# Batch 0's experts through the turned path, and five of the shared expert's low parts on VectorE

## The reference

```python
x = x + _L0_cond_ref(...)     # dense plus a low-rank mix over 8 experts
x = x + _L1_cond_ref(...)     # masked weights mixed by cond_8, plus bias
x = x + _L2_cond_ref(...)     # MoE: softmax, top 2 of 8, gated MLP 128 -> 512 -> 128, plus a shared expert
x = x + _L3_cond_ref(...)     # argmax expert, silu-gated MLP 128 -> 256 -> 128
# the gated MLP of the third layer:
def _gemma_mlp(x, gate_w, up_w, down_w):
    g = jnp.einsum('bsh,hi->bsi', x, gate_w)
    u = jnp.einsum('bsh,hi->bsi', x, up_w)
    return jnp.einsum('bsi,ih->bsh', jax.nn.gelu(g, approximate=True) * u, down_w)
```

## Time and profile before

| what | value |
|---|---|
| median of 3 runs | 81.27 us (81.17 to 81.83) |
| the profiled execution | 81.71 us, its span 80.3 us |
| PE busy | 76.7 us, 95% of the span |
| DVE, ACT, POOL busy | 52.1, 47.3, 45.4 us |
| bytes moved | 21.65 MB, mean 269 GB/s |

### The profile page before, as it was taken

How to read it: one execution, slowest core, us unless ns; L and a number is a source line. 1 busy time by engine, 2 the same in 40 slices (tenths; PEclk the granted TensorE clock), 3 DMA queues, 4 the chain that set the end, 5 groups by cost and what they waited for, 6 DMA issues and landing times.

```text
span 80.3 us, 1611 instructions
## 1 busy us (share of the span) xinstructions
PE 76.7 (95%) x500; PEld 69.4 (86%) x500; DVE 52.1 (65%) x116; ACT 47.3 (59%) x95; POOL 45.4 (57%) x44
## 2 busy tenths in 40 slices
PE   6999999999999999999995999999999999999990
PEld 6978998888888998999882989989989999999990
DVE  1489569869756637387697939499398465157371
ACT  6420796798855898637999059356450522168260
POOL 3021356298999999999999999995600000000000
PEclk9999999999999999999999999999999999999999
DMA  1999489999999993499988999999989789600202
GB/s 14 317 345 386 58 324 352 407 419 422 431 394 414 386 407 123 70 379 359 386 223 208 361 341 318 270 315 328 309 302 303 243 215 269 237 14 0 65 0 65
DMA packets 8791, 21.65 MB, mean 269 GB/s; under 512 B 976, under 2 KB 5200, under 8 KB 8784
## 3 DMA queue, kind: packets, MB, share of 16 engines
q1 hardware_dynamic: 8496, 20.77, 74.8%
q10 hardware_dynamic: 288, 0.79, 2.5%
HBM read 17.88 MB, written 0.52 MB: 229 GB/s over the span
## 4 chain that ended last, share of the span: by engine, by line
PE 87%; DMA 4%; SPq 2%; DVE 2%; ACT 1%; issue 1%
PE bank L961 18%; PE bank L934 9%; PE bank L976 8%; PE bank L991 5%; PE bank L897 5%; PE bank L913 5%; PE bank L905 5%; DMA x_t<-p 4%; PE bank L944 4%; PE bank L947 4%; PE bank L945 4%; PE bank L836 4%; PE bank L828 4%; SPq L259 2%; PE bank L921 2%; PE bank L923 2%
## 5 line engine op out<-in xcount | busy, mean ns | idle before, releaser
L418 ACT ACTIVATE gelu<-bank 128x512 f32<-128x512 f32 x24 | 14.2, 594 | 11.5 <-PE bank L947 6.9
L361 POOL TENSOR_TENSOR pair_low<-pair_w,wide_h 128x512 fp32r<-128x512 f32 x14 | 17.8, 1297 | 0.9 <-ACT wide_h L456 0.9
L691 DVE SCALAR_TENSOR_TENSOR hid<-gelu,wsel,bank 128x512 f32<-128x512 f32 x16 | 11.8, 736 | 7.6 <-PE bank L947 2.0
L366 POOL TENSOR_TENSOR hid_l<-hid,hid_h 128x512 fp32r<-128x512 f32 x8 | 10.3, 1295 | 2.0 <-ACT hid_h L469 1.9
L944 PE MATMUL bank<-wide_h,x_h 128*128 128x512 f32 x24 | 9.8, 409 | 0.0
L428 ACT ACTIVATE half<-bank,half_bias 128x128 f32<-128x128 f32 x12 | 3.8, 365 | 9.5 <-PE bank L976 6.5
L945 PE MATMUL bank<-wide_h,x_l 128*128 128x512 f32 x24 | 9.4, 390 | 0.0
L705 DVE STREAM_TRANSPOSE p<-hid 128x512 f32<-128x512 f32 x12 | 8.5, 712 | 0.8 <-DMA x_t<-p 0.4
L456 ACT ACTIVATE wide_h<-pair_w 128x512 fp32r<-128x512 f32 x14 | 8.1, 622 | 0.1
L689 DVE TENSOR_TENSOR hid<-gelu,bank 128x512 f32<-128x512 f32 x8 | 5.5, 686 | 3.8 <-POOL hid_l L366 2.7
L934 PE MATMUL bank<-x_t,pair_w 128*128 128x128 f32 x64 | 7.5, 275 | 0.0
(11 more groups left out here) (120 smaller groups left out, 162.9 us busy)
## 6 DMA issues: line engine op xcount, KB each, us to landing
pair_w<-in_skill SPq DMA_DIRECT2D x11, 768.0 KB, 7.4
w<-in_layer SPq DMA_DIRECT2D x6, 384.0 KB, 9.5
x_t<-p SPq DMA_DIRECT2D x12, 128.0 KB, 3.6
b_mix<-p SPq DMA_DIRECT2D x12, 128.0 KB, 4.3
shared_sb<-in_skill SPq DMA_DIRECT2D x1, 768.0 KB, 11.8
home_x<-in_skill SPq DMA_DIRECT2D x1, 768.0 KB, 12.6
home_h<-in_skill SPq DMA_DIRECT2D x1, 768.0 KB, 4.3
home_l<-in_skill SPq DMA_DIRECT2D x1, 768.0 KB, 6.3
```

The source lines that it names most:

```text
L361: pool.tensor_tensor(low_of(b, k)[:, m, :], w[:, m, :], wide_h[:, ring_at(b, k) % RING, m, :].bitcast(fp32), ALU.subtract).then_inc(wide_l ...
L366: pool.tensor_tensor(hid_l[:, k % 3, :], hid[:, k % 2, :], hid_h[:, k % 3, :].bitcast(fp32), ALU.subtract).then_inc(hid_low, 1)
L418: act.activation(gelu[:, n, :], ps[:, :], ACT.Gelu_apprx_tanh).then_inc(gelu_ready, 1)
L691: dve.scalar_tensor_tensor(hid[:, n, :], gelu[:, n, :], wsel[:, bass.DynSlice(weight, 1)], u_ps[n][:, :], ALU.mult, ALU.mult).then_inc(hid ...
```

## The change

`TURNED` becomes 0 to 6, so that batch 0's experts take the wide form, with its rounding, low parts, transposes and swap; batch 7 stays plain as it was. POOL makes the low parts of the shared expert's hidden values only for k = 0, 1, 2 (`POOL_LOW = 3`), DVE those for k = 3 to 7 (`hidden_rest`), each with a semaphore of its own. ACT rounds batch 0's and batch 1's weights during the shared expert, one part in each of seven places. The steps of batches 0 to 4 stand in another order on PE, ACT and DVE. On SP `swap(0)` stands ahead of the load of (4, 1), and `swap(1)` behind that one load, where it stood behind three before.

```diff
--- before.py
+++ after.py
@@ -24,7 +24,8 @@
 PAIRS, THIRD = 7, 3
 RING = 4
 IN_BANK = 4
-TURNED = range(1, B - 1)
+TURNED = range(B - 1)
+POOL_LOW = 3
 
 
 HEAD = 2 * C + B + B * E
@@ -280,10 +282,7 @@
 
                 pick(0, 0)
                 load(0, 0)
-                for b, k in ((1, 0), (0, 1), (1, 1)):
-                    pick(b, k)
-                    load(b, k)
-                for b, k in ((2, 0), (2, 1), (3, 0)):
+                for b, k in ((0, 1), (1, 0), (1, 1), (2, 0), (2, 1), (3, 0)):
                     pick(b, k)
                     load(b, k)
                 pick(3, 1)
@@ -298,15 +297,15 @@
                 for b in range(5, B):
                     pick(b, 0)
                     pick(b, 1)
+                swap(0)
                 sp.wait_ge(down_done, NSH)
                 load(4, 1)
+                swap(1)
                 load(5, 0)
                 load(5, 1)
-                swap(1)
-                sp.wait_ge(down_done, down_at(0, 0))
-                load(6, 0)
                 swap(2)
                 sp.wait_ge(down_done, down_at(0, 1))
+                load(6, 0)
                 load(6, 1)
                 swap(3)
                 sp.wait_ge(down_done, down_at(1, 0))
@@ -364,19 +363,15 @@
                 def hidden_low_part(k):
                     pool.wait_ge(hid_high, k + 1)
                     pool.tensor_tensor(hid_l[:, k % 3, :], hid[:, k % 2, :], hid_h[:, k % 3, :].bitcast(fp32),
-                                       ALU.subtract).then_inc(hid_low, 1)
-
-                for k in range(3):
-                    hidden_low_part(k)
-                wide_low_part(1, 0, 0)
-                hidden_low_part(3)
-                hidden_low_part(4)
-                wide_low_part(1, 0, 1)
-                hidden_low_part(5)
-                hidden_low_part(6)
-                wide_low_part(1, 1, 0)
-                hidden_low_part(7)
-                wide_low_part(1, 1, 1)
+                                       ALU.subtract).then_inc(hid_low_pool, 1)
+
+                wide_low_part(0, 0, 0)
+                hidden_low_part(0)
+                hidden_low_part(1)
+                wide_low_part(0, 0, 1)
+                hidden_low_part(2)
+                wide_low_part(0, 1, 0)
+                wide_low_part(0, 1, 1)
                 for b in TURNED[1:]:
                     for k in range(TOP_K):
                         for m in range(2):
@@ -468,40 +463,40 @@
                         act.wait_ge(down_done, k - 2)
                     act.activation(hid_h[:, k % 3, :], hid[:, k % 2, :], ACT.Copy).then_inc(hid_high, 1)
 
+                rounds = {1: (0, 0, 1), 3: (0, 1, 0), 4: (0, 1, 1), 5: (1, 0, 0), 6: (1, 0, 1), 7: (1, 1, 0)}
+                round_part(0, 0, 0)
                 gelu_step(0, 0, shg_ps[0])
                 for k in range(1, NSH):
                     gelu_step(k, k % 2, shg_ps[k % 3])
                     round_hidden(k - 1)
-                    if k in (3, 4):
-                        round_part(1, 0, k - 3)
-                    if k == NSH - 1:
-                        round_part(1, 1, 0)
+                    if k in rounds:
+                        round_part(*rounds[k])
+                expert_gelu(0, 0)
                 round_hidden(NSH - 1)
-                expert_gelu(0, 0)
                 round_part(1, 1, 1)
                 expert_gelu(0, 1)
                 round_pair(2, 0)
                 round_pair(2, 1)
                 expert_gelu(1, 0)
+                expert_gelu(1, 1)
                 round_pair(3, 0)
-                expert_gelu(1, 1)
+                expert_gelu(2, 0)
                 round_pair(3, 1)
-                expert_gelu(2, 0)
-                halve3(0)
-                tanh_step(0)
                 expert_gelu(2, 1)
                 round_pair(4, 0)
                 expert_gelu(3, 0)
                 round_pair(4, 1)
                 expert_gelu(3, 1)
+                halve3(0)
+                tanh_step(0)
+                expert_gelu(4, 0)
                 round_pair(5, 0)
-                expert_gelu(4, 0)
+                expert_gelu(4, 1)
                 round_pair(5, 1)
-                expert_gelu(4, 1)
-                round_pair(6, 0)
                 halve3(1)
                 tanh_step(1)
                 expert_gelu(5, 0)
+                round_pair(6, 0)
                 expert_gelu(5, 1)
                 round_pair(6, 1)
                 halve3(2)
@@ -681,15 +676,20 @@
 
                     dve.wait_ge(gelu_ready, k + 1)
                     dve.wait_ge(u_done, k + 1)
-                    if 2 <= k < NSH + 2:
-                        dve.wait_ge(hid_low, k - 1)
-                    elif NSH + 2 <= k < NSH + 4:
-                        dve.wait_ge(down_done, down_at(0, n))
+                    if 2 <= k < POOL_LOW + 2:
+                        dve.wait_ge(hid_low_pool, k - 1)
+                    elif POOL_LOW + 2 <= k < NSH + 2:
+                        dve.wait_ge(hid_low_dve, k - 1 - POOL_LOW)
                     if weight is None:
                         dve.tensor_tensor(hid[:, n, :], gelu[:, n, :], shu_ps(k)[:, :], ALU.mult).then_inc(hid_ready, 1)
                     else:
                         dve.scalar_tensor_tensor(hid[:, n, :], gelu[:, n, :], wsel[:, bass.DynSlice(weight, 1)],
                                                  u_ps[n][:, :], ALU.mult, ALU.mult).then_inc(hid_ready, 1)
+
+                def hidden_rest(k):
+                    dve.wait_ge(hid_high, k + 1)
+                    dve.tensor_tensor(hid_l[:, k % 3, :], hid[:, k % 2, :], hid_h[:, k % 3, :].bitcast(fp32),
+                                      ALU.subtract).then_inc(hid_low_dve, 1)
 
                 def add_shared(h):
                     dve.wait_ge(down_done, T * (h + 1))
@@ -778,31 +778,37 @@
                 share_sum()
                 bias_columns()
                 hidden(4, 0)
+                hidden_rest(3)
                 share_scale()
                 bias_halves()
                 hidden(5, 1)
+                hidden_rest(4)
                 norm_shares()
                 hidden(6, 0)
+                hidden_rest(5)
                 weight_part()
-                hidden(7, 1)
                 expert_weights()
                 settled()
-                expert_hidden(0, 0)
+                hidden(7, 1)
+                hidden_rest(6)
+                hidden(NSH, 0, 0)
+                hidden_rest(7)
+                turn(0, 0)
                 expert_hidden(0, 1)
                 add_shared(0)
                 add_shared(1)
                 expert_hidden(1, 0)
-                residual(0)
                 expert_hidden(1, 1)
                 expert_hidden(2, 0)
                 expert_hidden(2, 1)
-                layer3(0)
+                residual(0)
                 expert_hidden(3, 0)
                 expert_hidden(3, 1)
-                result(0, 0)
                 residual(1)
+                layer3(0)
                 expert_hidden(4, 0)
                 expert_hidden(4, 1)
+                result(0, 0)
                 residual(2)
                 layer3(1)
                 for b in range(5, B):
@@ -919,7 +925,10 @@
                         pe.wait_ge(sh_low, 3)
                     pe.matmul(sh_acc[h][:, :], shared_h[:, 2, C * t:C * (t + 1)], hid_h[:, n, :], start=(t == 0), stop=False)
                     pe.matmul(sh_acc[h][:, :], shared_l[:, 2, C * t:C * (t + 1)], hid_h[:, n, :], start=False, stop=False)
-                    pe.wait_ge(hid_low, k + 1)
+                    if k < POOL_LOW:
+                        pe.wait_ge(hid_low_pool, k + 1)
+                    else:
+                        pe.wait_ge(hid_low_dve, k + 1 - POOL_LOW)
                     pe.matmul(sh_acc[h][:, :], shared_h[:, 2, C * t:C * (t + 1)], hid_l[:, n, :], start=False, stop=(t == T - 1)
                               ).then_inc(down_done, 1)
 
@@ -1016,25 +1025,25 @@
                         shared_low(k, m)
                     if k >= 3:
                         shared_down(k - 3)
-                gate_up(0, 0)
-                gate_up(0, 1)
+                gate_up_wide(0, 0)
+                gate_up_wide(0, 1)
                 shared_down(NSH - 3)
                 shared_down(NSH - 2)
                 shared_down(NSH - 1)
                 gate_up_wide(1, 0)
+                gate_up_wide(1, 1)
+                gate_up_wide(2, 0)
+                gate_up_wide(2, 1)
                 down(0, 0)
                 down(0, 1)
-                gate_up_wide(1, 1)
-                layer3(0)
-                gate_up_wide(2, 0)
-                gate_up_wide(2, 1)
                 gate_up_wide(3, 0)
                 gate_up_wide(3, 1)
                 down(1, 0)
-                down3(0, 0)
                 down(1, 1)
+                layer3(0)
                 gate_up_wide(4, 0)
                 gate_up_wide(4, 1)
+                down3(0, 0)
                 down(2, 0)
                 down(2, 1)
                 layer3(1)
```

3 lines of the change are left out of this document (2 added, 1 removed).

## The result

The changed kernel takes 86.25 us (median of 4 runs, 85.21 to 87.54), the kernel before 81.55 beside it. The ratio is 1.048, with a 95% interval of 1.033 to 1.064: slower by about 5%, where I had forecast 83.2 us. The profiled execution is the one of 87.54 us, with a span of 86.2.

A forecast was written before the change was run, and what follows sets the result against it. PE, busy 95% of the span, was taken as the bound. Batch 7 starting 1.5 us later plus 0.4 at swap 3 gave +1.9 on 80.3; 83.6 profiled, less 0.44 for the median, made 83.2 us, range 80.2 to 84.6.

The forecast's parts named there:

- What PE gains, what DVE costs: Up to batch 7's start: PE could gain 2.2 us, but DVE's delays make batch 7 start 1.5 us later.
- POOL's wait for DVE: Beside DVE's low-part subtractions in the shared expert: POOL waits too, 0.55 us each, bounds 0 and 0.68.
- (a): Long DVE steps beside POOL cost next to nothing, their waits hide in idle time: 79.9 to 80.7 us, chance 0.22.
- (b): Half of the waits: `half_bias` and `wsel` find POOL between two parts: 80.5 to 82.1 us, chance 0.17.
- port: DVE and POOL steps reading SBUF wait for each other; waits in full: 82.2 to 84.4 us, chance 0.53.
- SP and the DMAs: Loads start 5.6 us later, so swap 3 lands late: 0.4 us taken, bounds 0 and 1.6.
- swaps 1 and 2 were paced by SP's issues and not by the DMAs before: At the loads and swaps: reason why part of the at most 1.6 us shortfall at swap 3 is made up.
- the loads stand queued ahead of the swaps and fill these holes: At the loads and swaps: reason for taking 0.4 us at swap 3, between 0 and 1.6.
- Rival (c): DMAs become the bound, with waits at swaps 0, 3 and 4: +3.8, 85.1 us, chance 0.08.

The follow-up runs named there:

- run 1: The changed kernel once more, unchanged, for a second profile: 87.27 us median (85.21 to 87.55).
- run 2: The changed kernel with the hidden values of k = 3, 4, 5 kept in PSUM: 85.28 us median (83.85 to 87.18).
- run 8: The changed kernel with the hidden values of k = 3 to 7 in PSUM and loads and swaps interleaved on SP: 83.21 us, ratio 1.017.
- run 9: The kernel before with only the change's order of loads and swaps on SP, batch 0 plain: 84.2 us median (82.17 to 86.8).
- run 11: The changed kernel with swap 2 put ahead of loads (5, 0) and (5, 1) on SP: 86.4 us median (84.51 to 87.23).
- runs 7: The changed kernel with swap 1 behind all three loads and swap 2 behind swap 1: 91.43 us (89.72 to 92.1).
- run 6: The changed kernel with loads (6, 0) and (6, 1) held on SP until swap 2 has landed: 89.51 us.
- 5: The changed kernel with loads and swaps interleaved on SP, one load ahead of each of swaps 0, 1 and 2: 85.4 us, ratio 1.043.
- runs 4: The changed kernel with all eight low parts of the hidden values back on POOL: 85.28 us, ratio 1.049.

## Why the prediction was wrong

**What PE gains, what DVE costs: right in its steps.** The steps of the sum held to 0.2 us: `hidden_rest(3)` forecast to end at 23.9, measured 23.87; `half_bias` 25.2, 25.05; `hidden_rest(4)` 27.0, 26.82; batch 0's start on PE 27.85, 27.70; `hidden(7)` 30.0, 30.12; `hidden_rest(7)` 33.1, 33.22; `turn(0, 1)` 35.1, 35.22; `down(0, 0)` 40.1, 40.12. In run 1's profile of the same kernel these steps lie 0.3 to 0.4 us earlier, so that hits closer than this are luck. POOL's wait for DVE, which no row of before showed, was taken as 0.55; three POOL parts took 4.25 instead of 3.78 with one `hid_l` between them, 0.47. (One reading was not exact: at 5.93 POOL still had a step that ended at 5.99.) By the rule of the Trainium skill ("SBUF — State Buffer", section "Who interferes with whom") both directions exclude each other; run 2 shows both, and that moving one operand to PSUM ends it. Rivals (a) and (b) fall with this. The sizes are about 1 us for three subtractions (run 2) and 2 us for five (run 8). What (a) promised for a port without cost, 79.9 to 80.7 us, did not come either: run 8 takes 83.21.

**SP and the DMAs: the step that failed.** I let the backlog show at swap 3 and took 0.4 us, between 0 and 1.6, and put the wait for swap 2 at nothing without working it out. Swap 2 is the one that held PE, for 2.4 us, 2.0 more than my 0.4, and swap 3 did not. That brings 83.2 to 85.2, and the full-clock executions took 85.21 to 86.56; none of them was profiled, so what lies between stays open. Two sentences of that step misled me. That "swaps 1 and 2 were paced by SP's issues and not by the DMAs before" says nothing of the new order: before, one load stood between swap 1 and swap 2, and swap 2 landed 4.0 to 4.5 us after its issue. The change puts two there, 1.5 MB, issued 0.4 and 1.1 us ahead of the swap; runs 9 (loads there, batch 0 plain: 6.4 us at most) and 11 (loads away: 3.3 us at most) show that they are what made it late. And "the loads stand queued ahead of the swaps and fill these holes": the holes in the changed kernel, from some 32 to 37 us, lie before any of these loads is issued, because load (4, 1) stands behind swap 0. I also priced a landing by its median, 4.0 us, though the row had 5.8 as its longest; by the median swap 2, its last transfer issued at 46.22, lands at 50.2, ahead of PE at 50.67, and by the longest at 52.0, a wait of 1.3. The Trainium skill ("DMA: Bandwidth & Descriptors", section "Queues, rings and completion order") says that one DMA is split over up to 16 of its row's rings, one ring per engine, that each engine takes its descriptors in ring order, and that its part of the completion lands only after its earlier writes. The packets of the changed kernel and of run 11, and the landings of runs 7 and 9, agree with that. That what counts is the fullest ring in front of the swap is inferred from it and from run 6; no run here shows a single ring.

**The clock: missing.** No term of the sum stood for it. Four of eight executions lost 1.7 us more to half clock after the gap, 2.25 and 2.28 us in the two profiled. Batch 7 in the profiled execution: 64.9 + 2.4 + 1.73 = 69.0, measured 69.22.

**Rival (c)**, the DMAs as the bound, 85.1 us, chance 0.08, was right in its cause, and in its time close to the 85.21 of the fastest executions, but by luck: it had its waits at swaps 0, 3 and 4, and none of them came. My range ended at 84.6, short of it. Run 11 shows why it deserved more: with the port's cost as it is, each order of loads and swaps tried (5, 7, 11) moves the wait to another swap, and batch 7 never starts before 66.26.

**Where the expected gain went.** PE has 2.2 us less to do by my count. In the changed kernel the port takes about 2 of them (run 8) and swap 2 takes 2.4. Without the port, swaps still take 1.8, and PE starts batch 0 1.4 us later than before; of that only the 0.46 for a bank is explained, and the rest stays open, as does whether an order of loads exists in which a turned batch 0 pays at all; the best seen is 1.7% slower than before.

## What to carry to other kernels

When loads and small urgent transfers share a queue, price the small one by what is issued in the 1 to 2 us in front of it (here its slowest DMA took 3.3 us with no load in that stretch, 3.7 to 5.8 with one of 768 KB, 6.2 to 7.7 with two, 7.9 with three), and check each of them, not the one that you expect to be last. A reordering that holds loads back behind a wait leaves the DMAs idle first and crowds them later. Before moving subtractions from GpSimd to VectorE, look whether GpSimd gets idle: with one operand in PSUM they cost 0.68 us beside it, with both in SBUF up to 1.7, and GpSimd pays too. And before a gain in one profile is credited to an edit, compare the starts of what lies ahead of it: the shared expert's first product started at 11.0 to 12.3 us in the profiles here.

## What the hardware showed that I had not expected

PE gaps of 2.25, 2.28, 2.47 and 4.16 us were followed by a granted clock of 0.50 (in the last it fell within the gap), for some 3 us, twice as long after the last (1.73 us lost after the first), and gaps of 0.95, 1.50 and 1.63 were not, in the executions profiled. The changed kernel's other four executions, none of them profiled, kept 1.00. In the kernel of run 9, which has a gap of 1.50 at full clock, other executions had a mean of 0.96 and 0.98. That small changes in landing times decide this is likely and not shown.

Swap 2's DMAs took up to 7.0 us even where the DMAs moved only 83 GB/s while it was waited for (run 6). If the 16 engines' backlogs were unequal, as I infer, the mean share hides it.

`half_bias` (128x16, one SBUF input) took 0.96 to 1.04 us beside a busy GpSimd wherever VectorE makes low parts, with the hidden values in PSUM too, and 0.32 to 0.33 in the kernel before and in runs 4 and 9. The forecast had this wait; what I had not expected is that it stays, with a single input, where the subtractions that have one operand in PSUM no longer wait.
